# Interleaving exponentials and half-precision copies on ScalarE in a cross-attention kernel

## The reference

```python
q = heads(x @ W_q);  k_t, v_t = heads(text @ W_k), heads(text @ W_v)
probs_t  = softmax(q @ k_t.T * scale)                      # over the 73 text tokens
text_out = probs_t @ v_t
qsem = l2norm(probs_t @ text);  sem = qsem @ l2norm(ip).T  # over 4 image tokens
probs_ip = softmax(q @ k_ip.T * scale + 0.5 * sem) * spatial_mask
out = concat_heads(text_out + probs_ip @ v_ip) @ W_out + b_out + x
```

## Time and profile before

| | before |
|---|---|
| median of 3 runs | 1028.56 us |
| profiled execution | 1025.27 us, span 1023.5 us |
| TensorE matmul busy | 973.4 us, 95% |
| VectorE busy | 802.7 us, 78% |
| ScalarE busy | 687.3 us, 67% |
| GpSimd busy | 640.7 us, 63% |
| DMA engines, q1 | 85.1% of 16 engines |

### The profile page before, as it was taken

One profiled execution on the slowest core, in us unless ns is written; L12 is line 12 of the kernel. 1 busy time (PEld: TensorE's weight loads), 2 busy tenths in 40 slices (PEclk: granted clock), 3 DMA queues, 4 the chain that ended last, 5 costly groups with the idle time before them and its releaser, 6 DMA issues.

```text
span 1023.5 us, 24720 instructions
## 1 busy us (share of the span) xinstructions
PE 973.4 (95%) x7604; PEld 797.0 (78%) x7604; DVE 802.7 (78%) x2401; ACT 687.3 (67%) x2315; POOL 640.7 (63%) x1899
## 2 busy tenths in 40 slices
PE   6997787999999999999999999999999999999988
PEld 4755566888877888888878888888878888888865
DVE  4366579888888888878888887888888888978872
ACT  1254668777777776776777777777767777776740
POOL 1112467767666766766676767677666767777761
PEclk9999989999999999999999999999999999999999
DMA  8845989889899898889899998788999889788883
GB/s 275 310 171 123 193 162 158 179 170 182 152 195 185 188 181 168 178 161 182 163 189 185 192 176 175 170 173 169 177 186 186 187 169 180 144 163 143 155 141 111
DMA packets 483872, 180.27 MB, mean 176 GB/s; under 512 B 449517, under 2 KB 461855, under 8 KB 483740
## 3 DMA queue, kind: packets, MB, share of 16 engines
q1 hardware_dynamic: 483708, 178.62, 85.1%
q10 hardware_dynamic: 32, 0.07, 0.0%
HBM read 42.34 MB, written 27.22 MB: 68 GB/s over the span
## 4 chain that ended last, share of the span: by engine, by line
PE 75%; DMA 5%; DVE 3%; SPq 3%; ACT 3%; issue 2%; POOL 1%; DVEq 0%; ACTq 0%
PE ps_Q L1254 25%; PE ps_O L1143 25%; PE ps_S L1164 12%; PE ps_U L1240 11%; DMA pts<-ph 4%; PE ps_M L1180 3%; ACT pr L924 2%; SPq L840 1%; ACT ph L936 1%; DMA x_in<-in_x_dram 1%; SPq L803 1%; SPq L813 1%; DVE pr L1085 0%; DVE bias L1046 0%; PE ps_U L1143 0%
## 5 line engine op out<-in xcount | busy, mean ns | idle before, releaser
L924 ACT ACTIVATE pr<-ps_S,bias 128x73 f32<-128x73 f32 x1280 | 288.9, 340 | 102.4 <-DVE bias L1046 100.9
L1006 POOL TENSOR_TENSOR ph<-pr,ph 128x220 f16<-128x220 f32 (+1 forms) x640 | 274.0, 460 | 129.7 <-ACT ph L936 129.6
L1254 PE MATMUL ps_Q<-xT,wq_hi 128*128 128x512 f32 x800 | 280.5, 416 | 5.5 <-DVE qT L1013 5.2
L1143 PE MATMUL ps_O<-wo_hi,aT 128*128 128x320 f16 x1220 | 279.6, 300 | 0.0
L936 ACT ACTIVATE ph<-pr 128x292 f16<-128x292 f32 x640 | 241.5, 500 | 0.4 <-DMA pts<-ph 0.3
L1143 PE MATMUL ps_O<-wo_lo,aT 128*128 128x320 f16 x610 | 182.7, 299 | 0.0
L1240 PE MATMUL ps_U<-xm,pts 128*128 128x110 f16 (+1 forms) x2560 | 159.7, 213 | 17.3 <-DMA pts<-ph 16.6
L1254 PEld LDWEIGHTS ps_Q<-xT,wq_hi 128*128 128x128 f32 x800 | 146.5, 191 | 33.4 <-DVE qT L1013 6.5
L1240 PEld LDWEIGHTS ps_U<-xm,pts 128*128 128x128 f16 (+1 forms) x2560 | 145.1, 98 | 34.8 <-issue 12.6
L1164 PEld LDWEIGHTS ps_S<-kbd,qT 128*128 128x128 f32 x960 | 152.1, 190 | 17.6 <-issue 2.4
L1164 PE MATMUL ps_S<-kbd,qT 128*128 128x308 f32 x960 | 163.9, 306 | 2.0 <-ACT pr L924 1.7
(11 more groups left out here) (214 smaller groups left out, 1285.1 us busy)
## 6 DMA issues: line engine op xcount, KB each, us to landing
out_dram<-x_in SPq DMA_DIRECT2D x64, 320.0 KB, 2.6
x_in<-in_x_dram SPq DMA_DIRECT2D x56, 320.0 KB, 3.2
pts<-ph SPq DMA_TRANSPOSE x320, 3.3
aT<-in_L_xattn_W_k_dram SPq DMA_DIRECT2D x5, 512.0 KB, 8.7
w_ip<-in_L_xattn_W_k_ip_dram SPq DMA_DIRECT2D x1, 2560.0 KB, 11.1
w_v<-in_L_xattn_W_v_dram SPq DMA_DIRECT2D x1, 2560.0 KB, 18.5
w_ip<-in_L_xattn_W_v_ip_dram SPq DMA_DIRECT2D x1, 2560.0 KB, 9.5
x_in<-in_x_dram SPq DMA_DIRECT2D x2, 1280.0 KB, 12.5
```

Source lines behind the costliest of these rows:

```text
L924: last = nc.scalar.activation(pr[p % P_RING][:, j, h, :], sc[:, j, h, 0:T], ACT.Exp, bias=bias[p % 2][:, j, h:h + 1], scale=SCALE)
L1006: nc.gpsimd.tensor_tensor(lo, full[:, :, t0:t1], one[:, :, 0, t0:t1], ALU.subtract).then_inc(pl_ready, 1)
L1143: last = nc.tensor.matmul(bank[:, 0:HALF], stationary, moving, start=(k, a, b_) == O_MMS[0], stop=(k, a, b_) == O_MMS[-1])
L1254: last = nc.tensor.matmul(ps_Q[:], wq[a][:, c, k * P:(k + 1) * P], xT[(CC * i + c) % XT_RING][b_][:], start=(c, a, b_) == Q_MMS[0], stop=( ...
```

## The change

In the body of a pair on ScalarE, the second loop over `j` is merged into the first. Before: four exponentials for `j` = 0, four for `j` = 1, two high copies for `j` = 0, two for `j` = 1. After: four exponentials for `j` = 0, the two high copies for `j` = 0, four exponentials for `j` = 1, the two high copies for `j` = 1. The wait for the cleared `ph` buffers (first two pairs only) moves ahead of the exponentials. No instruction is added, removed or resized, and no other engine's program is touched.

```diff
@@ -919,15 +919,14 @@
                     act.wait_ge(bias_ready, p + 1)
                     if p >= P_RING:
                         act.wait_ge(n2_done, p - P_RING + 1)
+                    if p < PH_RING:
+                        act.wait_ge(cleared, PH_RING)
                     for j in range(2):
                         for h in range(HG):
                             last = nc.scalar.activation(pr[p % P_RING][:, j, h, :], sc[:, j, h, 0:T], ACT.Exp,
                                                         bias=bias[p % 2][:, j, h:h + 1], scale=SCALE)
                         last.then_inc(p_ready, 1)
 
-                    if p < PH_RING:
-                        act.wait_ge(cleared, PH_RING)
-                    for j in range(2):
                         act.wait_ge(p_ready, 2 * p + j + 1)
                         if p >= PH_RING:
                             act.wait_ge(*ring(pts_loaded[j], p - PH_RING))
```

## The result

The changed kernel took 1036.69 us (median of 4 runs, 1036.25 to 1039.30) against 1025.91 us before (4 runs). The ratio is 1.0114, 95% interval 1.0089 to 1.0139. A later series on one chip, with 6 runs of the changed kernel and 16 of the kernel before, gave 1.0111 (1.0077 to 1.0145). The forecast of 1047 us stood on a median of 1028.56 us before the change; with the fourth run that median is 1025.91, so 2.65 of the 10.3 us of difference lie in the base. The profiled execution took 1036.25 us, span 1034.4 us.

What follows compares the result with a forecast made beforehand. TensorE was taken to bound the kernel. Stalls of 15.4 + 2 + 2.3 us less 1 us credited gave 18.7 us, forecasting 1047 us on the median of the runs shown, with an 8-in-10 range of 1033 to 1058 us.

Steps and rivals of the forecast that it cites:

- Bound by TensorE, with no gap to close: Steady part: TensorE busy 583.61 of 589.00 us, so a ScalarE change can save little and only open a gap.
- credited 1 us: Earlier first copies and transposes: 1 us taken off the loss for TensorE's shorter waits for transposes.
- The delay of 0.86 us: ScalarE within a pair: exponentials of the second 128 tokens end 0.86 us later, holding up TensorE's next second score half.
- The sequence 0, 1.02, 1.69, 2.71: ScalarE starts in a pair, in us: first exponentials, first copies, second exponentials, second copies; 0.05 us per wait for itself.
- The larger rival: ScalarE's wait for itself costs more than 0.05 us, up to 0.38: 1052 us at 0.15, 1066 towards the bound; chance 20%.
- The page's overlap: With the Trainium skill's 93 ns overlap of back-to-back ACTIVATEs: delay 0.96 us, whole loss some 24 us; left out of the sum.
- The middle, 15.4 us: Pairs 20 to 155: 44 of 136 margins lie below 0.92 us, and their shortfalls add up to 15.4 us.
- the rival "no change": Stalls are taken back by TensorE's queue and weight-load overlap, or by VectorE's slack: 1027 to 1031 us; chance 10%.
- Only even pairs, only those ending in 2, 6 and 8: TensorE's score groups: margins are tight behind these pairs; odd margins lie mostly between 1.5 and 2.1 us.
- The two ends: Stalls outside the middle: 2 us charged for the first two tiles, 2.3 us for the last three pairs.
- Wait of about 20 us, 45 to 55 times, each under 0.5 us: TensorE's score matmuls waiting for ScalarE's exponentials: a rise from 1.7 us to this, nearly all behind even pairs.
- Granted clock: TensorE's clock, 1.00 from 160 to 989 us: no fall expected, TensorE staying above 96% busy; clock rival's chance 2%.

Runs made afterwards that it cites:

- odd: New order in odd pairs only, old order in even pairs, against the kernel before: ratio 1.0018 (1.0002 to 1.0035).
- even: New order in even pairs only, old order in odd pairs, against the kernel before: ratio 1.0141 (1.0119 to 1.0164).
- spared: Kernel before with the new order except in the first 20 pairs, last 4 and pairs ending in 2, 6, 8: ratio 1.0026 (1.0003 to 1.0049).

## Why the prediction was right, and where it was off

The direction and the mechanism held. The time lay in the range, but the sum was too high: 18.7 us forecast, about 11 measured. Its largest term was too large and, as far as one profile of the kernel before can tell, the two terms for the ends were too small, so part of the error cancelled. By its steps:

- **Bound by TensorE, with no gap to close.** Right. The first transposes are issued earlier, and the waits for them fell by 4.6 us in the whole span (16.6 to 12.0), 3.3 of it in the first 200 us. I had credited 1 us and named "a few us at most". The first transposes of odd pairs were issued 0.56 us sooner and the second 0.41 (0.63 and 0.3 forecast), those of even pairs not at all (at most 0.25 forecast). How much of the 4.6 us became time is not shown: in the first 20 pairs 4.4 us of new stalls stand against 3.3 us less of this wait, and the stretch still grew by 3.2 us.
- **The delay of 0.86 us.** Measured 0.82. The sequence 0, 1.02, 1.69, 2.71 came out as 0, 0.99, 1.68, 2.65: ScalarE's wait for its own result cost 0.03 us, not 0.05, and second copies and exponentials were recorded slightly shorter. The larger rival, up to 0.38 us per wait, is refuted. Counted from the medians of the traces the delay is 0.81 us; with 0.81 + 0.05 = 0.86 in place of 0.92 the same margins give 12.8 us in place of 15.4.
- **The page's overlap.** By the 93 ns of the Trainium skill ("ScalarE: Activation LUTs", section "What ACT_TABLE_LOAD costs") the prediction's estimate of the delay was 0.96 us. The measurement decides: 0.82.
- **The middle, 15.4 us.** This is the term that was mis-sized: pairs 20 to 156 grew by only 8.1 us. It shrinks in three steps.
  - The smaller delay takes off 2.6 us (15.4 to 12.8), as just said.
  - The margins themselves moved. Stalls of 12.2 us were measured, 11.9 above those of before, against the 12.8 that the old margins give. The small sum hides a large shift between pairs. The margins were read from a trace in which GpSimd held up VectorE; in the new order pairs ending in 8 gained 0.3 us and stalled for 0.9 us in all instead of 3.1, while pairs ending in 2 lost about 0.1 us and stalled for 5.1 instead of 3.9. In that profile the low parts met another VectorE instruction ahead of pairs ending in 2, the one that makes `w_sem` (0.62 us in place of 0.23). In the second profile of the same kernel they did not (0.23 us there); it was the pairs ending in 6 that lost 0.2 us and stalled for 7.1 us instead of 5.2. The gain of pairs ending in 8 is in both profiles.
  - TensorE takes some back. Summed over the middle, the start-to-start times of the weight loads inside score groups grew by 10.4 us, so 1.5 of the 11.9 are made up within the group, where the loads behind a stall follow more closely. All other parts of its program together were 2.3 us quicker than before, in the values products (1.3), on the way into them (0.5) and into the `x` transposes (0.5). I had said a slip would not be made good; it is, by about a third (in the second profile 13.4 us of added stalls and 8.5 us of added time). That is the mechanism of the rival "no change", which had a true part.
- **Only even pairs, only those ending in 2, 6 and 8.** Shown by the odd, even and spared kernels.
- **The two ends.** Forecast 2 + 2.3. From pair 0 to pair 20 the changed kernel took 3.2 us more, and from pair 156 to the end 3.2 us more in the first profile. The second profile has 3.3 and 3.1 us, so these terms came out too small, not too large. But only one profile of the kernel before stands against them, and they are of the size of the scatter of the loop's start, so I can't call them measured to better than some 2 us. The first profile's span contains 3.5 us of an earlier loop start as well, which is why 8.1 + 3.2 + 3.2 = 14.5 stands against a span difference of 10.9. In the second profile the loop began as late as in the kernel before (96.5 against 96.4 us), and the span is 15.0 us longer.
- **Wait of about 20 us, 45 to 55 times, each under 0.5 us.** By my count over the score groups, 20.2 us in 51 stalls, 50 of them behind even pairs. Nine were longer than 0.5 us, the six at the two ends of the run up to 1.09 us. The profile's list has 16.9 us at the weight loads and 7.5 at the matmuls, which overlap.
- **Granted clock.** Full through the middle, as forecast; the row for the long stretch of the changed kernel (columns as in the earlier trace rows):

```profile
203.00:972.00 769.00, 762.51 (x6126) 630.10 (x6125) 629.62 (x1943) 587.15 (x1929) 533.84 (x1593) 1.00 0.90 172
```

## What to carry to other kernels

When one engine is full and the others have idle time, an order on a side engine is judged by the first consumer of each result, not by the engine's total. Here four exponentials had a consumer that in the tight pairs was due 0.5 us after them. The copies that were put ahead of them feed the transposes, and those landed 2 us and more (medians) before TensorE came to them. Read the margin of each consumer from the timeline, over a whole period of the schedule and not from one pair, and compare it with the delay; below the smallest margin a delay is free, and beyond it each place costs what the delay exceeds its margin by, less what the full engine takes back. Treat the margins themselves as good to some tenths of a microsecond, since they include contention that the new order will move.

## What was not expected of the hardware

GpSimd can hold up VectorE. A VectorE product of two small SBUF tiles (128x64) takes 0.17 us alone and 0.55 us when it starts beside a wide GpSimd subtraction (0.6 us); the product ends shortly after that instruction. In the kernel before, VectorE and then GpSimd at the step ahead of pair 138:

```profile
864.50 0.19 DVE L1088 RECIPROCAL rd<-nd 128x8 f32<-128x8 f32 x1
864.61 0.55 DVE L1092 TENSOR_TENSOR f<-nd,w_sem 128x64 f32<-128x64 f32 x1
865.08 0.75 DVE L1097 TENSOR_REDUCE n<-pr 128x8 f32<-128x584 f32 x1
```

```profile
864.49 0.87 POOL L1006 TENSOR_TENSOR ph<-pr,ph 128x220 f16<-128x220 f32 x2 [1.22 <-ACT ph L936]
```

The hold-up is not listed as idle time; it sits inside the recorded duration, as the same form with two different durations. Over the whole run of the kernel before, 48 of the 80 products began at least 0.06 us behind a low part that still had over 0.11 us to run. Each of the 48 ended 0.08 us after that low part's end (0.079 to 0.090). Where the low part began later than 0.06 us before the product, the product mostly took its 0.18 us (median of 19).

Not every VectorE instruction is held. The two small ones on lines 1101 and 1117, which also read two SBUF tiles, ended 0.08 us after such a low part, too. `w_sem`, which reads two as well, ended 0.03 us after it (40 times in the changed kernel). The reduction right behind the product ran at its usual 0.75 us although GpSimd was still at work. `attn` (0.41 us) and the update of `x_in` (0.54 us), which read PSUM, kept their durations beside it, too. This is what the traces show of the instructions in this kernel; no experiment varied the operands.
